# The steps of attention alone reordered in a fused linear-attention and mixture-of-experts kernel

## What is computed

```
mod = silu(c) @ wmod                      -> sa, ca, ga, sb, cb, gb per batch
h   = layernorm(x) * (1 + ca) + sa
q, k, v = h @ W_qkv, 16 heads of 16; rope on q and k
qf, kf  = elu(q * 16**-0.5) + 1, elu(k) + 1
kv  = sum over all 2048 rows of kf^T v;  k_sum = sum of kf       (per batch, head)
x   = x + ga * ((qf @ kv) / max(qf . k_sum, 1e-6)) @ W_out
h   = layernorm(x) * (1 + cb) + sb
x   = x + gb * moe(h)     8 experts, top 2, capacity 640 rows each, hidden 1024
```

## Time and profile before

| | us |
|---|---|
| median of 3 runs | 634.47 |
| lowest, highest | 633.26, 636.43 |
| the profiled execution, its own time | 630.97 |
| its span in the trace | 629.1 |

### The profile page before, as it was taken

How to read it: one execution, slowest core, us unless ns; L and a number is a source line. 1 busy time by engine, 2 the same in 40 slices (tenths; PEclk the granted TensorE clock), 3 DMA queues, 4 the chain that set the end, 5 groups by cost and what they waited for, 6 DMA issues and landing times.

```text
span 629.1 us, 12912 instructions
## 1 busy us (share of the span) xinstructions
PE 559.4 (89%) x3895; PEld 519.9 (83%) x3895; DVE 453.0 (72%) x1357; ACT 322.9 (51%) x718; POOL 269.9 (43%) x406
## 2 busy tenths in 40 slices
PE   5999999999888532499999999999999999999993
PEld 4587779988677311399899999999999999999993
DVE  4688799998678887787577577677676776666441
ACT  4688878886334434045445454445445444454331
POOL 5788857776667600403044062070170260431321
PEclk9999999999889855599999999999999999999997
DMA  6322458644546470333637347258066174360312
GB/s 169 106 67 85 123 176 241 220 137 141 168 143 202 158 215 0 86 101 101 185 84 145 102 97 170 64 110 209 21 124 188 52 138 140 89 139 6 37 19 25
DMA packets 92480, 75.28 MB, mean 120 GB/s; under 512 B 12156, under 2 KB 89094, under 8 KB 92424
## 3 DMA queue, kind: packets, MB, share of 16 engines
q1 hardware_dynamic: 82344, 57.39, 30.5%
q0 software_dynamic: 8992, 15.90, 13.6%
q10 hardware_dynamic: 1088, 1.31, 0.7%
HBM read 52.41 MB, written 22.16 MB: 119 GB/s over the span
## 4 chain that ended last, share of the span: by engine, by line
PE 65%; DVE 10%; issue 4%; ACT 3%; POOL 2%; DMA 2%; SPq 0%; POOLq 0%; DVEq 0%; ACTq 0%
PE bank L1587 29%; PE bank L1601 14%; PE bank L1622 4%; PE bank L1369 4%; PE bank L1494 3%; PE bank L1637 2%; PE bank L1480 1%; PE bank L1563 1%; ACT side L698 1%; PE bank L1406 1%; DMA w_raw<-wd 1%; DVE st L1005 1%; DVE x L1003 1%; PE bank L1449 1%; PE bank L1544 1%
## 5 line engine op out<-in xcount | busy, mean ns | idle before, releaser
L556 POOL DMA_INDIRECT xg<-h_rows,g_idx x40 | 44.1, 1103 | 236.5 <-DVE g_idx L1186 226.7
L1587 PE MATMUL bank<-xT_h,w_h 128*128 128x320 f32 x448 | 139.9, 312 | 1.5 <-DVE xT_l L1215 1.5
L1587 PE MATMUL bank<-xT_l,w_h 128*128 128x320 f32 x448 | 138.4, 309 | 0.0
L1587 PE MATMUL bank<-xT_h,w_l 128*128 128x320 f32 x448 | 138.2, 309 | 0.0
L733 ACT CAST hid_h<-hid 128x320 fp32r<-128x320 f32 x112 | 51.5, 460 | 86.6 <-DVE hid L1243 86.6
L566 POOL DMA_INDIRECT out<-yo,s_idx x40 | 67.1, 1676 | 59.8 <-DVE yo L1308 26.7
L1587 PEld LDWEIGHTS bank<-xT_h,w_h 128*128 128x128 f32 x448 | 84.6, 189 | 2.2 <-issue 1.4
L729 ACT ACTIVATE act_g<-bank 128x320 f32<-128x320 f32 x112 | 49.0, 437 | 70.0 <-PE bank L1587 69.1
L1587 PEld LDWEIGHTS bank<-xT_l,w_h 128*128 128x128 f32 x448 | 84.5, 189 | 0.0
L1587 PEld LDWEIGHTS bank<-xT_h,w_l 128*128 128x128 f32 x448 | 84.4, 188 | 0.0
L1248 DVE TENSOR_TENSOR hid_l<-hid,hid_h 128x320 fp32r<-128x320 f32 x112 | 54.9, 490 | 36.5 <-ACT hid_h L733 36.1
(11 more groups left out here) (223 smaller groups left out, 1299.6 us busy)
## 6 DMA issues: line engine op xcount, KB each, us to landing
w_raw<-wg SPq DMA_DIRECT2D x32, 256.0 KB, 3.7
w_raw<-wu SPq DMA_DIRECT2D x32, 256.0 KB, 4.9
w_raw<-wd SPq DMA_DIRECT2D x16, 512.0 KB, 6.0
x_in<-x SPq DMA_DIRECT2D x32, 128.0 KB, 2.1
q_store<-qT SPq DMA_DIRECT2D x32, 128.0 KB, 2.1
q_in<-q_store SPq DMA_DIRECT2D x32, 128.0 KB, 2.2
x_re<-x SPq DMA_DIRECT2D x32, 128.0 KB, 2.1
out<-x SPq DMA_DIRECT2D x32, 128.0 KB, 2.1
```

The costliest lines, as they stand in the source:

```text
L556: nc.gpsimd.indirect_dma_start(out=xg[par][:, a, :], out_offset=None, in_=h2_rows, in_offset=bass.IndirectOffsetOnAxis(ap=g_idx[par][:, a: ...
L1587: last = MM(bank[2 * h + m][:, 0:HCAP], W[i][:, f, at:at + P], XT[j][:, k, cols], start=n == 0, stop=n == 3 * KC - 1)
```

## The change

`alone` begins at step 34. The second state is copied right behind att of step 33. The choices of group 0 move to steps 36 to 44, those of group 1 to steps 44 to 49; ScalarE's exponentials stand one step behind their part 0 (steps 37 and 45). On VectorE the places (L883) move from behind att to behind x2's statistics (L1005), in every step that has both; choices move from the step's end and from ahead of att to the place behind the aggregation (L841), ahead of L846. In steps 47 and 48 (`SECOND_CHOICE + 3`, `+ 4`) two parts of a choice follow each other.

```diff
--- before.py
+++ after.py
@@ -115,14 +115,14 @@
     return 2 <= s.rep < TB
 
 
-FIRST_CHOICE = NT + 6
-SECOND_CHOICE = NT + LAG - 5
-EX_STEPS = (FIRST_CHOICE, SECOND_CHOICE)
+FIRST_CHOICE = NT + 4
+SECOND_CHOICE = NT + LAG - 6
+EX_STEPS = (FIRST_CHOICE + 1, SECOND_CHOICE + 1)
 
 
 def alone(s):
 
-    return s.rep >= NT + 6
+    return s.rep >= NT + 2
 
 
 def stages(s):
@@ -863,6 +863,14 @@
 
             TT, RED = V.tensor_tensor, V.tensor_reduce
 
+            def state(b):
+
+                dve.wait_ge(kv_d, (b + 1) * TB)
+                V.tensor_tensor(kvb[b][:, :, 0:P], kv_ps[:, :, 0:P],
+                                blk[:, 0:P].unsqueeze(1).to_broadcast([P, KC, P]), ALU.mult)
+                V.tensor_tensor(kvb[b][:, :, P:], kv_ps[:, :, P:P + 1].to_broadcast([P, KC, HC]),
+                                blk[:, P:].unsqueeze(1).to_broadcast([P, KC, HC]), ALU.mult).then_inc(kvb_d, 1)
+
             def finish_logits(s):
 
                 t = s.t(-LAG - 3)
@@ -982,16 +990,14 @@
                     V.reciprocal(den_r[:, :, :], den_m[:, :, :]).then_inc(drec, 1)
                     if on["logit"]:
                         pick_values(s.t(o - 3))
-                    if SECOND_CHOICE < s.rep < SECOND_CHOICE + 5:
-                        choice(1, 2 * (s.rep - SECOND_CHOICE) - 1)
                     dve.wait_ge(drec, s.t(o + 1))
                     wait(dve, tr_o, s.t(o))
                     V.tensor_tensor(att[:, :].rearrange("p (c h d) -> p c h d", c=KC, d=HD),
                                     o_ps[:, :, 0:P].rearrange("p c (h d) -> p c h d", d=HD),
                                     den_r[:, :, :].unsqueeze(3).to_broadcast([P, KC, HC, HD]), ALU.mult)\
                         .then_inc(att_d, 1)
-                    if on["logit"]:
-                        pick_places(s.t(o - 3))
+                    if s.rep == NT + 1:
+                        state(1)
                 if on["proj"]:
                     o = -LAG - 1
                     t = s.t(o)
@@ -1003,16 +1009,30 @@
                     V.tensor_tensor(x2[t % 3][:, :], y_ps, x_re[s.par(o)][:, :], ALU.add).then_inc(x2_d, 1)
                     dve.wait_ge(x2_d, s.t(o + 1))
                     V.bn_stats(st2[:, :], x2[t % 3][:, :]).then_inc(bn2, 1)
-                    if not between(Step(s.k, s.j, s.rep + 1)):
-                        variance2(s, o)
+                if on["logit"] and on["att"]:
+                    pick_places(s.t(-LAG - 3))
+                if on["proj"] and not between(Step(s.k, s.j, s.rep + 1)):
+                    variance(st2, mv2, bn2, ag2, s.t(-LAG))
+                    if 0 <= s.rep - FIRST_CHOICE < CHOICE:
+                        choice(0, s.rep - FIRST_CHOICE)
+                    if 0 <= s.rep - SECOND_CHOICE < 3:
+                        choice(1, s.rep - SECOND_CHOICE)
+                    if s.rep == SECOND_CHOICE + 3:
+                        choice(1, 3)
+                        choice(1, 4)
+                    if s.rep == SECOND_CHOICE + 4:
+                        choice(1, 5)
+                        choice(1, 6)
+                    if s.rep == SECOND_CHOICE + 5:
+                        choice(1, 7)
+                    wait(dve, scale2, s.t(-LAG - 2))
+                    finish_stats(mv2, nm2[s.par(-LAG - 1)], ve2[s.par(-LAG - 1)], ag2, stat2, s.t(-LAG))
+                    if s.rep == SECOND_CHOICE + 5:
+                        choice(1, 8)
                 if on["logit"] and not on["att"]:
                     finish_logits(s)
                     pick_values(s.t(-LAG - 3))
                     pick_places(s.t(-LAG - 3))
-                if 0 <= s.rep - FIRST_CHOICE < CHOICE:
-                    choice(0, s.rep - FIRST_CHOICE)
-                if SECOND_CHOICE <= s.rep < SECOND_CHOICE + 5:
-                    choice(1, 2 * (s.rep - SECOND_CHOICE))
                 if s.rep == NT + 5:
                     with nc.allow_low_precision(reason="zeros and ones"):
                         RED(own_q[:, :], ident.rearrange("p (q r) -> p q r", q=Q), AX, ALU.add)
@@ -1027,13 +1047,8 @@
                     router_centred()
                 if GATE_STEP <= s.rep < GATE_STEP + 8:
                     mod_rows(s.rep - GATE_STEP + 1)
-                if s.rep in (TB + 1, NT + 1):
-                    b = s.rep // TB - 1
-                    dve.wait_ge(kv_d, s.rep - 1)
-                    V.tensor_tensor(kvb[b][:, :, 0:P], kv_ps[:, :, 0:P],
-                                    blk[:, 0:P].unsqueeze(1).to_broadcast([P, KC, P]), ALU.mult)
-                    V.tensor_tensor(kvb[b][:, :, P:], kv_ps[:, :, P:P + 1].to_broadcast([P, KC, HC]),
-                                    blk[:, P:].unsqueeze(1).to_broadcast([P, KC, HC]), ALU.mult).then_inc(kvb_d, 1)
+                if s.rep == TB + 1:
+                    state(0)
 
             steps(dve, step, ATT)
```

## The result

| | changed | before | ratio, 95% interval |
|---|---|---|---|
| median of 6 runs each | 629.88 us | 635.09 us | 0.9917 [0.9891, 0.9943] |
| the profiled execution (its span) | 629.77 (628.0) | 630.97 (629.1) | |
| a second comparison, other batch | 625.55 | 631.47 | 0.9909 [0.9892, 0.9925] |

The change is faster by 5.2 us, 0.8%: 629.88 lies in the wider range that was forecast, 623.8 to 630.5, but above the forecast's own, 625 to 628.5, and 3.2 above the 626.7. Two questions follow. Why 5 to 6 us and not 7.8? And why are the two profiled spans only 1.1 apart? In the changed file VectorE's lines from L866 on and TensorE's are numbered anew: L1466 is L1481, L1480 is L1495, L1406 is L1421, L1494 is L1509, L1504 is L1519; att is L995, x2 L1009.

A forecast was written before the change was run, and what follows sets the result against it. From step 33 a TensorE-ScalarE ring of 2.57 us per step, tied with VectorE, bounds the kernel. Savings 2.1 + 1.4 + 0.3 + 3.0 + 1.0 = 7.8 us from 634.47 gave 626.7, range 625 to 628.5, wider 623.8 to 630.5.

The forecast's parts named there:

- The ring: Steps 33 to 50: TensorE's y and ScalarE's copy, xn and attT set 2.57 us per undisturbed step, VectorE tied.
- rival D: The gain ends before the end, or one wait stays: within 3 us of now, 633; chance 0.08.
- The second state: Step 33 to 34: copied behind att, y to y falls from 4.58 to 2.49, 2.1 us saved.
- The clock: Step 34 to 35: without TensorE's stall the clock stays up, 3.98 becomes 2.57, 1.4 us saved.
- rival B: Gaps put TensorE at half clock in all 16 steps from 34: 646.4 us; chance 0.04.
- The own bank: Steps 35 to 38: L1466 no longer waits for x2, 8.24 becomes 7.96, 0.3 us saved.
- The first exponential: Steps 38 to 40: exponential a step later, ScalarE's wait for VectorE gone, 8.17 becomes 5.14, 3.0 us saved.
- The queue of SP: Steps 40 to 45: one L1480 wait of 0.32 us for its q tile stays, 0 saved.
- rival C: SP's transfers fall behind, L1480 waits 0.32 in eight steps: 5.6 saved, 628.9 us; chance 0.07.
- The second exponential: Step 45 to 46: 3.78 becomes 2.82, 1.0 us saved.
- VectorE's order: VectorE's chain inside a step falls from 2.57 to about 2.3 us; worth nothing where the ring binds.
- rival A: VectorE becomes the bound; step 37 costs 0.3 to 0.6 more, double steps 0.3 each: 6.6 saved, 627.9 us; chance 0.17.

The follow-up runs named there:

- the changed one, again: The changed kernel, without edit, profiled once more: 624.2 us (span 622.5).
- the second profile of before: The kernel before, without edit, profiled once more: 630.75 us (span 629.0).
- the state alone: The kernel before with only the second state moved right behind att of step 33: ratio 0.9955 to the kernel before.
- three buffers: The changed kernel with three buffers for the q tile, loaded two steps ahead: ratio 0.9925 to the kernel before.
- this order alone: The kernel before with only VectorE's order inside a step changed: ratio 0.9990 to the kernel before.
- the exponentials stand in their own step: The changed kernel with the exponentials in the step of their part 0 (36 and 44): ratio 0.9944 to the kernel before.
- the late state: The changed kernel with the second state back at the end of step 33: ratio 0.9942 to the kernel before.

## Why the prediction was right, and where it was not

**The ring.** Right: undisturbed steps take 2.55 to 2.58 from y to y in every profile, and the chain of VectorE, shortened as it was, does not bring them lower. The gain reaches the end: y(50) to the end is 419.9 and 420.95 in the kernel before and 420.6 in the changed one, again; its first profile, with the stall in the experts, has 424.5. So rival D is out.

**The second state.** Forecast 2.49 for the step, measured 2.53 in both profiles. 2.05 saved of 2.1 against the earlier trace rows; 1.67 against the second profile of before, where the step took 4.20 at full clock: 0.38 of the 4.58 were already the clock's.

**The clock.** This is the term that was mis-sized: "So 2.57, 1.4 saved", and another 1.15 (3.72 less 2.57) inside the 3.0 of the first exponential. Of the 1.4 only 0.88 is the clock. At full clock the second profile of before still takes 3.10 from y(34) to y(35), and the state alone, with 0.91 idle in place of 1.27, has 3.23: TensorE waits for x2 there (0.63 in both), and it is the own bank that takes this away. So the step "Without the 1.27 us of idle TensorE the stage should look like 183 to 198 us" gave the clock 0.53 of its 1.4 that is a wait. With the 0.38 in the state's term the sum holds 1.26 for the first fall and 1.15 for the second, 2.4 in all, and took both as certain. They came in four of six and in two of five profiles; weighed so, they are worth some 0.8 and 0.5. One profiled execution shows that a stall can cost the clock, not that it does. Of rival B nothing happened: the clock of the changed kernel is 1.00 in both its profiles from 156 to 200. Nor did the rule of the Trainium skill ("TensorE: Matmul & The Clock Gate", Part 4: PE-mode transpose), by which the full clock does not engage for transposes, hold for this mix, in which four of 16 matmuls of a step are transposes.

**The own bank.** Forecast 7.96 for 35 to 38; the first profile has 3.17 + 2.55 + 2.77 = 8.49, where before it was 8.24: 0.25 lost and not 0.3 saved, since a q tile was late by 0.6. Without that (three buffers) it is 7.91, as forecast. What the bank gives in 33 to 34 was in the state's term, and what it gives in 34 to 35 in the clock's.

**The first exponential.** No wait, as forecast. "Covered by half a microsecond" is the step that failed: y(39) was 0.34 late. att of step 38 ended 1.74 after y(38), near the reckoned 1.72 (171.7 less a y(38) of 169.98), but the cover was measured to ScalarE's attT alone. On TensorE L1481, L1495 and L1421 stand between att and y and take 1.11 (173.37 to 174.48): att must end 1.4 after y, not 1.7.

**The queue of SP** (steps 40 to 45, rival C). One wait of 0.32 kept; measured in the changed kernel 0.5 to 0.6 in step 36 and 0.45 to 0.66 in step 42, in both profiles; 0.6 to 0.9 more than the sum had. The other two-buffer kernels whose steps run at speed from 34 on have the same two. Rival C named the mechanism and put it in eight steps; it is in two, each behind one or more long issues on SP. That these make the tile late is not shown; with the tile loaded a step earlier they do no harm.

**The second exponential.** Forecast 2.82, measured 2.71: 1.07 saved of 1.0.

**VectorE's order** was taken as worth nothing once the ring binds. In the whole change no run takes it out, so its share there is not measured; alone it gives 1.3 in the steps named above, since it shortens the waits which the other parts remove. Where the exponentials stand in their own step it shows: the wait for the first over is 1.00 with this order alone, not 1.59. Of rival A the 0.34 behind step 37 came true, the 0.3 for each double step did not: steps 46 to 50 take 2.57 each.

**The sum.** The time alone, 5.2 saved, would fit the 5.6 of rival C better than the forecast's 7.8, though the tile was late in two steps and not in eight: that 629.88 falls into the wider range is no proof of the working. The stage was forecast at 44.4 and took 45.53 and 45.17; the rest is the stage of before, which is 52.20 in one profile and 49.76 in the other. Without the clock the two undisturbed profiles differ by 49.76 less 45.17 = 4.6 in the stage, in parts 1.67, 0.42, 1.54, -0.19, 1.14 and 0.01. With the falls at their frequency some 1.3 come on top: 5.9, where the times say 5.2 [3.6, 6.9] and 5.7 [4.7, 6.8]. That is near, but the frequencies come from 11 stalls, and the interval of the first comparison alone is 3.3 wide. The 7.8 was the difference of one disturbed execution of before from an ideal one after.

## What to carry to other kernels

Find the ring that sets the undisturbed step, and price every stall as the step's length less that: the step of the second state, the three steps of the own bank without their late q tile, and the step of the second exponential came out within 0.11 us. A long step can hold two losses at once, here the clock and the wait for x2; look for the second before one cause is given the whole. What a stall does to the clock belongs in the range, not in the sum, until a second profile shows it again. The slack of an engine must be taken to the instruction that the ring ends in, through everything queued in front of that on its engine.

## What the runs showed that was not expected

TensorE's clock fell to the lower level (0.50 to 0.54) after single idle times of 1.1 to 2.0 us in a stage where it is otherwise four fifths busy (1.27 in the earlier trace rows, 1.97 before the q tile of step 42 with the late state). Of two executions of the kernel before, with the same idle times, it fell in one and not in the other. Each profile has two to five issues on SP of 0.6 to 2.1 us between 158 and 205 us where nearly all others take 0.3 to 0.5; with two buffers, TensorE waited 0.15 to 2.0 for q tiles loaded near some of them, and near others not at all. And the stall of 5.1 to 5.3 us on ScalarE with no releaser in the program, together with 0.4 to 0.6 us more in each of four experts, was in all four profiles of one batch and in the changed kernel's first, in none of the other nine, and cost about 4 us from y(50) to the end.
